# A four-layer graph network: router logits inside the normalizations, one stage for a graph layer's batch norms, attention vectors as weight columns

## The chip, the cores and the metric

The kernel runs on one core of one Trainium2 chip. The metric is the device time of one execution in microseconds (us), the median of three runs. TensorE does matrix products, VectorE (DVE in the profile), ScalarE (ACT) and GpSimd (POOL) do elementwise work, SyncE (SP) issues transfers; each runs its own list of instructions, and they wait for each other on semaphores.

## The reference, cut to what matters

The program has four layers on 3125 nodes of 256 numbers and 50000 edges. Each layer is a graph part with a mixing part, and then a feed-forward part. Only these steps are touched:

```python
def _layernorm(x, axis=-1, eps=1e-05):
    m = jnp.mean(x, axis=axis, keepdims=True)
    v = jnp.var(x, axis=axis, keepdims=True)
    return (x - m) / jnp.sqrt(v + eps)

# feed-forward of layers 0, 1, 2 (16, 8 and 8 experts): the input is _layernorm(x)
logits = xt @ Wr + br                 # then softmax, top 2, 1 or 2
# layer 2 only: the normalized rows are normalized once more for the experts
xn = (xt - mu) * jax.lax.rsqrt(var + LN_EPS)

# graph part of layer 2, x is the normalized input
y = agg + eps_weight * x
h = jax.nn.relu(_batchnorm(y @ w1.T, gamma1, beta1))     # mean and variance over the nodes
y = jax.nn.relu(_batchnorm((h @ w2.T) * n_norm, gamma_h, beta_h))
y = y + x

# graph part of layer 3
h = x @ W
s, t = h @ a[:f_out], h @ a[f_out:]
```

## The kernel before, in words

The nodes are cut into NT = 25 tiles of P = 125 rows. `R.X` holds the running sum with a node per partition, `R.XN` its normalized copy, `R.XNT` the same turned by TensorE, so that 128 of the 256 columns (KC = 2 chunks) lie on the partitions. All of these are f32. The program is a row of stages. Most of them open a `Block`, at whose end all five engines meet at a barrier; inside a block each engine follows its own list in the order written, and nothing passes a barrier.

- `normalize_stage` (L463): DVE takes `bn_stats` of each tile (or is given `moments` by the stage before), ACT takes one square root, DVE writes 25 normalized tiles (L495), TensorE turns each with two transposes (L517), ACT copies them to `XNT` (L505).
- `router_stage` (L2225) first calls `rows_stage` (L526), which loads the gate weights (L554), multiplies tile by tile (L595) and lets DVE add the bias (L2246). A second block then chooses experts, nearly all of it on DVE, with one exponential on ACT (L2284).
- Layer 2's feed-forward calls `normalize_stage` a second time (f2ln2, on `R.XN` in place, without turning) after the router and before the rows are stored for the experts (L2450).
- `isomorphism_graph_layer` (L3219): after the edge stage, one block adds eps times the input (L3240), `turn_stage` turns the sums, `batchnorm_product_stage` runs twice (loads, products of 500 columns at L3155, copy or scaling at L3172 and L3170, then 50 `bn_stats` at L3178, then the batch norm and relu on ACT in two instructions of 3125 columns, L3204), and `rows_stage` turns the result back by a product with a unit matrix and adds it and the input to `R.X` (L3268, L3270).
- `attention_graph_layer` (L3309): `rows_stage` multiplies by W, and its `finish` (L3325 to L3332) copies 256 columns out of PSUM, multiplies them twice and sums them twice on DVE, per tile; two transfers per tile store the result (L561).

Matrix products of f32 appear twice in the trace, as two weight loads (PEld) and two multiplications (PE); transposes appear once.

## Time and profile before

| | before |
|---|---|
| median of 3 runs | 6918.84 us (6914.28 to 6926.26) |
| time of the profiled execution | 6917.47 us |
| its span, first to last instruction | 6915.8 us |
| mean granted TensorE clock | 0.823 |
| busy: PE, DVE, POOL, ACT | 61%, 51%, 44%, 27% |

The profiled execution is the one whose trace is read below; its time is 1.7 us more than its span, and 1.4 us less than the median. A granted clock of 1.00 is 2.4 GHz and of 0.50 is 1.2 GHz, the two levels that TensorE has; a value between is a mean over time.

### The profile page before, as it was taken

To read this page: it belongs to the slowest core of one execution; us is meant where nothing else is said; L and a number is where in the kernel's file an instruction comes from. 1 tells how busy PE (TensorE), PEld (TensorE's weight loads), DVE (VectorE), ACT (ScalarE), POOL (GpSimd) and SP (SyncE) were. 2 spreads that over 40 slices of the span, in tenths; PEclk is the share of its full clock that TensorE was granted. 3 is DMA by queue.
4 is the path that set the end of the run, shared out by engine and by line. 5 is a ranking of instruction groups with operands and counts; after the bars stand their busy time and mean duration, and the time that the engine had idled before them with its cause. 6 is when DMAs were issued, how large, how long until landed. Compare 5 with 4: busy or idle time off the path is not lost. (4 is left out here: it accounts for less than half of the span.)

```text
span 6915.8 us, 68089 instructions
## 1 busy us (share of the span) xinstructions
PE 4214.5 (61%) x17738; PEld 2954.0 (43%) x17738; DVE 3498.8 (51%) x8540; ACT 1896.6 (27%) x4978; POOL 3013.4 (44%) x3029
## 2 busy tenths in 40 slices
PE   0023567777777499476665592555445994577659
PEld 0000334444444277134444482344325883344436
DVE  7700478888888621636554214643343113555447
ACT  0000046666666222013343121000011221244321
POOL 0777023333333055326666364666502443466520
PEclk9985688888888599689877696777676997799879
DMA  1001023333334166343336232333603663333220
GB/s 40 3 18 25 11 81 97 98 99 99 98 97 97 37 192 196 97 146 89 90 89 84 73 97 85 91 92 91 74 13 101 191 192 89 89 86 87 78 44 19
DMA packets 364930, 600.63 MB, mean 87 GB/s; under 512 B 122830, under 2 KB 248896, under 8 KB 361176
## 3 DMA queue, kind: packets, MB, share of 16 engines
q0 software_dynamic: 162496, 359.47, 21.7%
q1 hardware_dynamic: 202060, 236.87, 11.1%
q8 instruction: 151, 2.47, 0.1%
q14 instruction: 223, 1.82, 0.1%
HBM read 517.26 MB, written 78.63 MB: 86 GB/s over the span
## 5 line engine op out<-in xcount | busy, mean ns | idle before, releaser
L1675 POOL DMA_INDIRECT g0e_got<-g_table,g0e_rc x496 | 475.5, 959 | 1079.9 <-DVEq L1835 728.9
L1428 POOL DMA_INDIRECT g1e_got<-g_table,g1e_rc x496 | 492.4, 993 | 457.8 <-DMA g1e_rc<-rec_dst 218.6
L1428 POOL DMA_INDIRECT g2e_got<-g_table,g2e_rc x496 | 480.5, 969 | 279.9 <-issue 140.5
L1428 POOL DMA_INDIRECT g3e_got<-g_table,g3e_rc x440 | 432.6, 983 | 356.5 <-issue 114.0
L1484 PE MATMUL g2e_pa<-g2e_got,g2e_placew 128*125 128x256 f32 x992 | 340.2, 505 | 369.9 <-DVEq L1586 261.7
L1763 PE MATMUL g0e_spread<-g0e_expanded,g0e_by_tile 128*125 128x512 bf16 x992 | 418.7, 514 | 176.8 <-ACT g0e_spaced L1712 141.1
L2640 PE MATMUL f_p<-f_w2s,f_hid 128*128 128x256 f32 (+1 forms) x2176 | 498.8, 386 | 39.4 <-ACT f_hid L2660 31.9
L257 POOL DMA_INDIRECT rec_dst<-bydst_rc,bydst_sloti x391 | 400.1, 1023 | 274.9 <-DVEq L450 150.3
L2629 PE MATMUL f_p<-f_xt,f_w1s 128*128 128x256 f32 (+1 forms) x2176 | 495.6, 385 | 29.2 <-issue 18.7
L1712 ACT ACTIVATE g0e_spaced<-g0e_spread 125x512 bf16<-125x512 f32 x992 | 499.4, 624 | 21.0 <-issue 7.7
L2660 ACT ACTIVATE f_hid<-f_p,f_b1s 128x256 f32<-128x256 f32 (+1 forms) x544 | 248.7, 472 | 850.4 <-PE f_p L2629 442.4
L2629 PEld LDWEIGHTS f_p<-f_xt,f_w1s 128*128 128x128 f32 x2176 | 417.8, 193 | 96.9 <-issue 20.9
L2640 PEld LDWEIGHTS f_p<-f_w2s,f_hid 128*128 128x128 f32 (+1 forms) x2176 | 408.2, 191 | 116.4 <-ACT f_hid L2660 61.0
L1484 PEld LDWEIGHTS g2e_pa<-g2e_got,g2e_placew 128*125 128x125 f32 x992 | 240.4, 254 | 454.2 <-issue 408.2
L257 POOL DMA_INDIRECT rec_src<-bysrc_rc,bysrc_sloti x391 | 381.0, 974 | 119.2 <-issue 119.2
L1484 PE MATMUL g3e_pa<-g3e_got,g3e_placew 128*125 128x257 f32 x880 | 269.4, 459 | 185.6 <-ACTq L1448 119.7
L2595 POOL DMA_INDIRECT f_got<-f_rows,f_of_slot x176 | 186.1, 1058 | 386.5 <-PE f_pt L2617 290.1
L1818 DVE TENSOR_TENSOR g0e_spaced<-g0e_spaced 125x2048 bf16<-125x2048 bf16 x496 | 326.9, 659 | 54.4 <-ACT g0e_spaced L1712 7.7
L1769 PE MATMUL g0e_pa<-g0e_msg,g0e_place 128*125 128x272 f32 x992 | 335.6, 496 | 3.0 <-DVEq L1853 3.0
L1484 PE MATMUL g1e_pa<-g1e_got,g1e_placew 128*125 128x256 f32 x992 | 308.2, 465 | 11.3 <-issue 6.7
L1763 PEld LDWEIGHTS g0e_spread<-g0e_expanded,g0e_by_tile 128*125 128x125 bf16 x992 | 140.6, 152 | 406.2 <-ACT g0e_spaced L1712 367.5
L517 PE MATMUL ln_pt<-identf,XN 125*128 125x125 f32 x200 | 44.5, 367 | 440.9 <-DVE XN L495 363.2
(664 smaller groups left out, 8247.9 us busy)
## 6 DMA issues: line engine op xcount, KB each, us to landing
f_w1s<-in_L_ffn_W SPq DMA_DIRECT2D x32, 1024.0 KB
f_w2s<-in_L_ffn_W SPq DMA_DIRECT2D x32, 1024.0 KB
g_table<-g1t_out SPq DMA_DIRECT2D x25, 896.0 KB
f_w1s<-in_L_ffn_w SPq DMA_DIRECT2D x40, 512.0 KB
f_w2s<-in_L_ffn_w SPq DMA_DIRECT2D x40, 512.0 KB
f_results<-f_y SPq DMA_DIRECT2D x88, 224.0 KB
f_b2s<-in_L_ffn_b SPq DMA_DIRECT2D x80, 128.0 KB
f_w1s<-in_L_ffn_w SPq DMA_DIRECT2D x9, 1024.0 KB
```

Of the source, the lines that this page charges most:

```text
L257: pool.indirect_dma_start(self.rec, bass.IndirectOffsetOnAxis(self.sloti[:, c:c + 1], 0), self.rc[:, c, :], None).then_inc(scattered, 16)
L1428: pool.indirect_dma_start(got[:, g % GOTS, j, :], None, table, bass.IndirectOffsetOnAxis(rc[:, g * GT + j, idx:idx + 1], 0))\
L1484: last = pe.matmul(pa[x % adds][:, 0:width], placew[:, g % 3, j, :], got[:, g % GOTS, j, 0:width], start=(j % each == 0), stop=(j % each = ...
L1675: pool.indirect_dma_start(got[:, s, j, :], None, table, bass.IndirectOffsetOnAxis(rc[:, sl, j, R_IDX:R_IDX + 1], 0)).then_inc(got_in[s], 16)
L1712: act.activation(spaced[:, j, h:h + 4, :], spread[:, u % 3, :].rearrange("p (h e) -> p h e", e=128), ACT.Copy).then_inc(copied, 1)
L1763: pe.matmul(spread[:, u % 3, :], by_tile[:, j, :], expanded[:, s % 2, h:h + 4, :], start=True, stop=True).then_inc(spread_out, 1)
L1769: last = pe.matmul(pa[:, 0:W], place[:, s, j, :], msg[:, s % 2, j, :], start=(j == 0), stop=(j == GT - 1))
L1818: dve.tensor_tensor(a, a, b, ALU.max)
L2595: pool.indirect_dma_start(got[:, s % 2, j, :], None, rows, bass.IndirectOffsetOnAxis(of_slot[:, s * TJ + j:s * TJ + j + 1], 0))\
L2629: last = pe.matmul(p1[n % 4][:, 0:TS], w1s[:, weights_of(s), c, f * 128:(f + 1) * 128], xt[:, s % 2, c, :], start=(c == 0), stop=(c == KC ...
L2640: last = pe.matmul(p2[n % 2][:, 0:D], hid[:, f, j * RP:(j + 1) * RP], w2s[:, weights_of(s), f, :], start=(f == 0), stop=(f == NF - 1))
L2660: act.activation(hid[:, f, :], p1[n % 4][:, 0:TS], func, bias=b1s[:, weights_of(s), f:f + 1])\
```

## The change

Four places are rewritten.

1. `normalize_stage` can be given a `Logits` object. It then loads the gate weights itself, and TensorE multiplies tile t-2 by them right after it has turned tile t. All 25 results stay in one PSUM bank, and DVE adds the bias to all of them in one instruction. `router_stage` no longer calls `rows_stage`.
2. For layer 2 `normalize_stage` also gets `moments`, so that it takes no statistics of `R.X`, and an `Again` object: after the last normalized tile DVE takes the statistics of the normalized rows. In the router block DVE and ACT turn them into a scale and a shift, and ACT normalizes the 25 tiles a second time while DVE goes on with the router. The second `normalize_stage` (f2ln2) is gone.
3. `isomorphism_tail` does in one block what six did: TensorE turns the sums, DVE adds eps times `XNT` while it takes them out of PSUM (`join`), products, copies and `bn_stats` follow chunk by chunk (six chunks of 500 columns, one of 125), the batch norms run on ACT per chunk, and each chunk goes on to the next product at once. The result is turned back by transposes, DVE adds it to `R.X` and takes the `bn_stats` for the next normalization. The input `R.XN` is added to `R.X` by one GpSimd instruction on 6400 columns.
4. `attention_rows_stage` multiplies W by the two attention vectors once, on DVE, and puts the two sums beside W as columns 257 and 258. Per tile ACT copies 256 columns and DVE copies two single columns.

The core of the diff; removed functions stand above in full.

```diff
@@ normalize_stage
+            if again is not None:
+                dve.drain()
+                for t in range(NT):
+                    dve.bn_stats(again.stats[:, t, :], node_tile(dst, t))
+                dve.drain()
+                for t in range(NT):
+                    dve.bn_aggr(again.mv[:, t, :], again.stats[:, t, :])
+            if logits is not None:
+                E = logits.experts
+                dve.wait_ge(logits.loaded, 32)
+                dve.wait_ge(logits.multiplied, NT)
+                dve.tensor_tensor(logits.lg[:, :, :], lp[:, 0:NT * E].rearrange("p (t e) -> p t e", e=E),
+                                  logits.gb[:, :].rearrange("p (a e) -> p a e", a=1).broadcast_to([P, NT, E]), ALU.add)
...
+            def project(t):
+                pe.wait_ge(evacuated, t + 1)
+                for c in range(KC):
+                    last = pe.matmul(lp[:, t * logits.experts:(t + 1) * logits.experts], R.XNT[:, c, t * P:(t + 1) * P],
+                                     logits.gw[:, c, :], start=(c == 0), stop=(c == KC - 1))
+                last.then_inc(logits.multiplied, 1)
...
+                    turn(t)
+                    if logits is not None and t >= 2:
+                        if t == 2:
+                            pe.wait_ge(logits.loaded, 32)
+                        project(t - 2)
@@ router_stage, scalar
             act.drain().then_inc(exped, 1)
+            if again is not None:
+                act.wait_ge(again.have_var, 1)
+                act.activation(again.std[:, :], again.std[:, :], ACT.Sqrt).then_inc(again.rooted, 1)
+                act.wait_ge(again.ready, 1)
+                for t in range(NT):
+                    act.activation(node_tile(R.XN, t), node_tile(R.XN, t), ACT.Identity, bias=again.shift[:, t:t + 1],
+                                   scale=again.std[:, t:t + 1])
@@ router_stage, vector
             dve.drain().then_inc(shifted, 1)
+            if again is not None:
+                dve.tensor_scalar(again.std[:, :], again.mv[:, :, 1], LN_EPS, None, ALU.add)
+                dve.drain().then_inc(again.have_var, 1)
+                dve.wait_ge(again.rooted, 1)
+                dve.reciprocal(again.std[:, :], again.std[:, :])
+                dve.drain()
+                dve.scalar_tensor_tensor(out=again.shift[:, :], in0=again.mv[:, :, 0], scalar=-1.0, in1=again.std[:, :],
+                                         op0=ALU.mult, op1=ALU.mult)
+                dve.drain().then_inc(again.ready, 1)
             dve.wait_ge(exped, 1)
@@ isomorphism_tail (new)
+        @block.gpsimd
+        def _(pool):
+            pool.tensor_tensor(R.X[:, :], R.X[:, :], R.XN[:, :], ALU.add).then_inc(xn_added, 1)
...
+            turn(0)
+            pe.wait_ge(first_in, 48)
+            for q in range(NQ):
+                if q + 1 < NQ:
+                    turn(q + 1)
+                pe.wait_ge(joined, tiles(q)[-1] + 1)
+                if q >= 2:
+                    pe.wait_ge(a_copied, q - 1)
+                product(0, yt, q, a_made)
...
+            for q in range(NQ):
+                at = columns(q)
+                act.wait_ge(a_made, q + 1)
+                act.activation(zt[:, :, at], ps[q % 2][:, :, 0:at.stop - at.start], ACT.Copy).then_inc(a_copied, 1)
...
+            def join(q):
+                for t in tiles(q):
+                    rows = slice(t * P, (t + 1) * P)
+                    dve.wait_ge(turned, t + 1)
+                    dve.scalar_tensor_tensor(out=yt[:, :, rows], in0=R.XNT[:, :, rows], scalar=eps[:, 0:1],
+                                             in1=pt[t % 2][:, 0:KC * P].rearrange("k (c p) -> k c p", p=P),
+                                             op0=ALU.mult, op1=ALU.add).then_inc(joined, 1)
...
+            dve.wait_ge(eps_in, 16)
+            join(0)
+            for q in range(NQ):
+                if q + 1 < NQ:
+                    join(q + 1)
+                dve.wait_ge(a_copied, q + 1)
+                for m in range(KC):
+                    for t in tiles(q):
+                        dve.bn_stats(stats[:, 0, m, t, :], zt[:, m, t * P:(t + 1) * P])
...
+            moments_of(1)
+            dve.wait_ge(xn_added, 1)
+            for t in range(NT):
+                x = node_tile(R.X, t)
+                dve.wait_ge(rows_turned, t + 1)
+                dve.tensor_tensor(x, x, bk[t % 2][:, 0:D], ALU.add)
+                dve.drain().then_inc(rows_added, 1)
+                dve.bn_stats(row_stats[:, t, :], x)
@@ attention_rows_stage (new)
+        def _(act):
+            for t in range(NT):
+                act.wait_ge(multiplied, t + 1)
+                if t >= OUTS:
+                    act.wait_ge(stored[t % OUTS], 32 * (t // OUTS))
+                act.activation(out[:, t % OUTS, 0:D], ps[t % OUTS][:, 0:D], ACT.Copy).then_inc(copied, 1)
...
+            for k in range(2):
+                dve.tensor_tensor(tmp[:, k, :, :], w[:, :, 0:D],
+                                  av[:, k, :].rearrange("p (a e) -> p a e", a=1).broadcast_to([128, KC, D]), ALU.mult)
+            dve.drain()
+            for k in range(2):
+                dve.tensor_reduce(w[:, :, D + k], tmp[:, k, :, :], AX.X, ALU.add)
+            dve.drain().then_inc(folded, 1)
+            for t in range(NT):
+                dve.wait_ge(copied, t + 1)
+                if t >= OUTS:
+                    dve.wait_ge(stored[t % OUTS], 32 * (t // OUTS))
+                dve.tensor_copy(out[:, t % OUTS, D + 1:D + 2], ps[t % OUTS][:, D:D + 1])
+                dve.tensor_copy(S[:, t:t + 1], ps[t % OUTS][:, D + 1:D + 2])
+                dve.drain().then_inc(taken, 1)
```

How the order changes is seen on three lists. First TensorE in layer 0's normalization and router, before: `f0ln_pt` are the transposes, `f0r_lg_ps` the logits, the branches are ends and starts of blocks.

```order
L517 MATMUL f0ln_pt<-identf,XN 128x125 x50
L465 UNCONDITIONAL_BRANCH
L575 UNCONDITIONAL_BRANCH
L595 MATMUL f0r_lg_ps<-f0r_gw,XNT 125x16 x50
L533 UNCONDITIONAL_BRANCH
```

The same place after the change, from its start (`f0ln_lp` are the logits):

```order
L560 MATMUL f0ln_pt<-identf,XN 128x125 x6
L567 MATMUL f0ln_lp<-f0l_gw,XNT 125x16 x2
L560 MATMUL f0ln_pt<-identf,XN 128x125 x2
L567 MATMUL f0ln_lp<-f0l_gw,XNT 125x16 x2
L560 MATMUL f0ln_pt<-identf,XN 128x125 x2
```

Two transposes and two products now take turns in one block, tile by tile, where before all transposes stood ahead of a barrier and all products behind it.

Second, TensorE after layer 2's edge stage, after the change: `g2p_pt` are the transposes of the sums, `g2p_ps` the products. Before, the 50 transposes (L3092) made a block of their own ahead of all products.

```order
L3224 MATMUL g2p_pt<-identf,g_acc 128x125 x16
L3232 MATMUL g2p_ps<-g2p_yt,g2p_ws 128x500 x4
L3224 MATMUL g2p_pt<-identf,g_acc 128x125 x8
L3232 MATMUL g2p_ps<-g2p_yt,g2p_ws 128x500 x4
L3224 MATMUL g2p_pt<-identf,g_acc 128x125 x8
```

Third, DVE in the same place after the change; the first row of each pair is the joins, the second the statistics of a chunk of the product.

```order
L3285 SCALAR_TENSOR_TENSOR g2p_yt<-XNT,g2p_eps,g2p_pt 128x2x125 x8
L3313 BN_STATS g2p_stats<-g2p_zt 128x6 x8
L3285 SCALAR_TENSOR_TENSOR g2p_yt<-XNT,g2p_eps,g2p_pt 128x2x125 x4
L3313 BN_STATS g2p_stats<-g2p_zt 128x6 x8
L3285 SCALAR_TENSOR_TENSOR g2p_yt<-XNT,g2p_eps,g2p_pt 128x2x125 x4
```

The joins of chunk q+2 now stand behind the statistics of chunk q on DVE, while the transposes of chunk q+2 stand ahead of the product of chunk q+1 on TensorE.

## Rows read from the trace of the kernel before

**Rows 1.** Busy time by stretch: start:end us, length, busy (instructions), granted clock.

```profile
core 0: us, PE busy (x) PEld busy (x) DVE busy (x) ACT busy (x) POOL busy (x), PEclk, DMA share, GB/s
2329.00:2334.00 5.00, 4.74 (x23) 3.90 (x24) 5.00 (x17) 3.70 (x10) 0.00 (x0) 0.50 0.00 0
2342.70:2364.00 21.30, 21.18 (x100) 21.07 (x100) 4.24 (x25) 0.00 (x0) 0.00 (x0) 0.50 0.00 0
...
5028.00:5048.00 20.00, 18.83 (x51) 8.81 (x49) 7.96 (x14) 0.00 (x0) 0.00 (x0) 1.00 0.00 0
5882.00:5930.00 48.00, 26.10 (x76) 15.32 (x76) 40.80 (x133) 0.00 (x0) 0.00 (x0) 0.85 0.21 60
```

**Rows 2.** Timeline of layer 0's normalization and logits: start, length, instructions, [idle before].

```profile
2329.26 6.00 PEld L517 LDWEIGHTS f0ln_pt<-identf,XN 125*128 125x128 f32 x30 [15.75 <-DVE XN L495]
...
2342.74 21.18 PE L595 MATMUL f0r_lg_ps<-f0r_gw,XNT 128*125 128x16 f32 x100 [3.94 <-DMA f0r_gb<-in_L_ffn_gate_b]
...
2363.96 0.17 DVE L2246 TENSOR_TENSOR f0r_lg<-f0r_lg_ps,f0r_gb 125x16 f32<-125x16 f32 x1 [0.67 <-PE f0r_lg_ps L595]
```

**Rows 3.** Timeline of layer 2's graph part behind the edge stage, into the normalization.

```profile
5000.07 9.99 DVE L3240 SCALAR_TENSOR_TENSOR g_acc<-XN,g_eps,g_acc  x25 [4.16 <-DMA g_eps<-in_L_gnn_eps_weight]
...
5023.25 23.58 PE L3155 MATMUL g2a_ps<-g_yt,g2a_ws 128*128 x56 [4.12 <-DVEq L3164]
...
5029.33 1.26 DVE L3172 COPY g_zt<-g2a_ps 128x500 f32 x2 [19.27 <-PE g2a_ps L3155]
...
5032.68 1.27 DVE L3172 COPY g_zt<-g2a_ps 128x500 f32 x2 [2.08 <-PE g2a_ps L3155]
...
5048.59 0.54 DVE L3178 BATCH_NORM_STATS2 g2a_stats<-g_zt  x2 [0.47 <-issue]
...
5068.05 0.83 DVE L3183 BATCH_NORM_AGGREGATE g2a_mv<-g2a_stats 128x2 f32<-128x150 f32 x1
...
5070.36 5.87 ACT L3204 ACTIVATE g_zt<-g_zt,g2a_shift,g2a_scale 128x3125 f32<-128x3125 f32 x2 [0.97 <-DVEq L3196]
...
5166.41 0.42 DVE L3268 TENSOR_TENSOR X<-X,g2back_ps 125x256 f32<-125x256 f32 x1
5166.91 0.43 DVE L3270 TENSOR_TENSOR X<-X,XN 125x256 f32<-125x256 f32 x1
...
5169.56 8.26 DVE L485 BATCH_NORM_STATS2 f2ln_stats<-X 125x6 f32<-125x256 f32 x25 [1.18 <-PEq L3583]
...
5180.85 8.16 DVE L495 TENSOR_SCALAR XN<-X,f2ln_mv,f2ln_std 125x256 f32<-125x256 f32 x25
```

**Rows 4.** Timeline of layer 2's router and the second normalization behind it.

```profile
5221.48 0.23 ACT L2284 ACTIVATE f_weight<-f2r_diff 125x25 f32<-125x25 f32 x1 [4.16 <-DVEq L2329]
...
5221.76 0.18 DVE L2333 TENSOR_SCALAR f_weight<-f_weight 125x25 f32<-125x25 f32 x1 [0.34 <-ACTq L2287]
...
5222.94 0.64 DVE L2344 COPY f2r_totals<-f2r_ps 125x200 f32<-125x200 f32 x2 [0.34 <-PE f2r_ps L2296]
...
5231.84 1.28 ACT L501 ACT_TABLE_LOAD   x1 [10.13 <-PEq L2232]
...
5251.35 5.50 SPq L2450 DMA_DIRECT2D f_rows<-XN  x2
```

**Rows 5.** ACT and POOL groups: line engine op, shapes, count | busy, mean ns | idle.

```profile
L3456 ACT ACTIVATE f_hid<-f_p,f_b1s 128x500 f32<-128x500 f32 x48 | 32.4, 677 | 120.0 <-PE f_p L3434 120.0
...
L786 ACT ACTIVATE m_k<-m_sq,m_rk 125x256 f32<-125x256 f32 x25 | 12.5, 499 | 0.0
...
L318 POOL IOTA sort_gid<- 128x496 f32 x1 | 0.6, 550 | 17.3 <-POOLq L3558 17.3
```

**Rows 6.** Instructions of line L561: count, min/median/max ns, first to last start.

```profile
L561 SPq DMA_DIRECT2D g_table<-g3h_out x50: 308/354/393, 5878.2 to 5929.3; - x50
```

**Rows 7.** Timeline of layer 3's product with W and of the stage behind it.

```profile
5873.97 7.39 PE L595 MATMUL g3h_ps<-g_w,XNT 128*125 128x258 f32 x24 [6.08 <-DMA g_a<-in_L_gnn_a]
...
5931.36 1.77 SPq L1414 DMA_DIRECT2D g3e_rc<-rec_src  x4
```

More of the change, by code:

```diff
@@ L478, in normalize_stage, with _ @@
             "have_var", "have_std", "normed", "turned", "evacuated"))
+        if logits is not None:
+            lp = ctx.enter_context(nc.psum_tensor(f"{name}_lp", [P, 512], F32))
         block = open_block(nc, R, ctx)
+        if logits is not None:
+            @block.sync
+            def _(sp):
+                sp.dma_start(logits.gw[:, :, :], chunks_of(logits.gate_w, logits.experts)).then_inc(logits.loaded, 16)
+                sp.dma_start(logits.gb[:, :], row_of(logits.gate_b, P)).then_inc(logits.loaded, 16)
+                sp.wait_ge(logits.loaded, 32)
         @block.vector
@@ L2237, in sem @@
             return nc.alloc_semaphore(f"{name}_{n}")
-        gw = sb("gw", [128, KC, experts])
-        gb = sb("gb", [P, experts])
-        lg = sb("lg", [P, NT * experts])
-        lgv = lg[:, :].rearrange("p (t e) -> p t e", e=experts)
+        lgv = logits.lg[:, :, :]
         best = sb("best", [P, top, NT])
-        def finish(dve, t, ps, out):
-            dve.tensor_tensor(lg[:, ds(t * experts, experts)], ps[:, 0:experts], gb[:, :], ALU.add)
-        rows_stage(nc, R, f"{name}_lg", gw[:, :, :], experts, finish,
-                   loads=[(gw[:, :, :], chunks_of(gate_w, experts)), (gb[:, :], row_of(gate_b, P))])
         items = top * NT
@@ L3305, in third_feed_forward, with attention_rows_stage, sb, _ @@
         routed_experts_stage(nc, R, "f2", F2, a["L2_ffn_W1"], a["L2_ffn_b1"], a["L2_ffn_W2"], a["L2_ffn_b2"], route,
                              ACT.Gelu, ThirdSettle(nc, ctx, R, route, moments), ln=a["L2_ffn_ln"], spare=spare, share=5)
+def attention_rows_stage(nc, R, a, S, table):
+    with ExitStack() as ctx:
+        def sb(n, shape):
+            return ctx.enter_context(nc.sbuf_tensor(f"g3h_{n}", shape, F32))
+        w, av, tmp = sb("w", [128, KC, D + 2]), sb("av", [128, 2, D]), sb("tmp", [128, 2, KC, D])
+        out = sb("out", [P, OUTS, D + 2])
+        ps = [ctx.enter_context(nc.psum_tensor(f"g3h_ps{k}", [P, 512], F32)) for k in range(OUTS)]
+        loaded, folded, multiplied, copied, taken = (nc.alloc_semaphore(f"g3h_{n}") for n in (
+            "loaded", "folded", "multiplied", "copied", "taken"))
+        stored = [nc.alloc_semaphore(f"g3h_stored{k}") for k in range(OUTS)]
+        block = ctx.enter_context(nc.Block())
+        @block.sync
+        def _(sp):
+            sp.dma_start(w[:, :, 0:D], chunks_of(a["L3_gnn_W"], D)).then_inc(loaded, 16)
+            sp.dma_start(av[:, 0, :], row_of(a["L3_gnn_a"][D:2 * D], 128)).then_inc(loaded, 16)
+            sp.dma_start(av[:, 1, :], row_of(a["L3_gnn_a"][0:D], 128)).then_inc(loaded, 16)
+            sp.wait_ge(loaded, 48)
+            for t in range(NT):
+                sp.wait_ge(taken, t + 1)
+                for own in spans(P):
+                    sp.dma_start(table[t * P:(t + 1) * P, :][own, :], out[own, t % OUTS, :]).then_inc(stored[t % OUTS], 16)
+            for k in range(OUTS):
+                sp.wait_ge(stored[k], 32 * len(range(k, NT, OUTS)))
+        @block.tensor
+        def _(pe):
+            pe.wait_ge(folded, 1)
+            for t in range(NT):
+                if t >= OUTS:
+                    pe.wait_ge(taken, t - OUTS + 1)
+                for c in range(KC):
+                    last = pe.matmul(ps[t % OUTS][:, 0:D + 2], R.XNT[:, c, t * P:(t + 1) * P], w[:, c, :], start=(c == 0),
+                                     stop=(c == KC - 1))
+                last.then_inc(multiplied, 1)
+        @block.scalar
+        def _(act):
+            for t in range(NT):
+                act.wait_ge(multiplied, t + 1)
+                if t >= OUTS:
+                    act.wait_ge(stored[t % OUTS], 32 * (t // OUTS))
+                act.activation(out[:, t % OUTS, 0:D], ps[t % OUTS][:, 0:D], ACT.Copy).then_inc(copied, 1)
+        @block.vector
+        def _(dve):
+            dve.memset(out[:, :, D:D + 1], 1.0)
+            dve.wait_ge(loaded, 48)
+            for k in range(2):
+                dve.tensor_tensor(tmp[:, k, :, :], w[:, :, 0:D],
+                                  av[:, k, :].rearrange("p (a e) -> p a e", a=1).broadcast_to([128, KC, D]), ALU.mult)
+            dve.drain()
+            for k in range(2):
+                dve.tensor_reduce(w[:, :, D + k], tmp[:, k, :, :], AX.X, ALU.add)
+            dve.drain().then_inc(folded, 1)
+            for t in range(NT):
+                dve.wait_ge(copied, t + 1)
+                if t >= OUTS:
+                    dve.wait_ge(stored[t % OUTS], 32 * (t // OUTS))
+                dve.tensor_copy(out[:, t % OUTS, D + 1:D + 2], ps[t % OUTS][:, D:D + 1])
+                dve.tensor_copy(S[:, t:t + 1], ps[t % OUTS][:, D + 1:D + 2])
+                dve.drain().then_inc(taken, 1)
```

341 lines of the change are left out of this document (160 added, 181 removed).

## The prediction

> **What bounds the kernel now.** No engine is busy for more than 61% of the span, and stages end at barriers that nothing passes, so the share of an engine says little: a change is worth what it takes off the chain inside its own stage. I read, in this order, the busy times by stretch for the clock [rows 1], then the timeline of each of the four places [rows 2, 3, 4, 7], then groups by line for prices that these places do not show [rows 5, 6]. The reader is to see three kinds of lost time. In the logits TensorE is never idle, yet it runs at 1.2 GHz (granted 0.50) over 21.3 us [rows 1]. Behind layer 2's edge stage one engine works while the others stand: product, then statistics, then relu, then the next product. In layer 3's product with W, TensorE is busy for 26.1 of 48 us and DVE for 40.8 [rows 1]: DVE is the bound.
>
> The sum is made against the profiled execution, 6917.5 us, which is 1.4 us under the median.
>
> **Term 1, logits in the normalization (three layers).** Layer 0 before: first transpose at 2329.26, last bias add ends at 2364.13, so 34.9 us, with the wait for the gate weights and a barrier inside [rows 2]. After: one stream on TensorE of 50 transposes and 100 load-and-multiply pairs (the f32 products count twice). At 1.2 GHz a transpose costs 6.00/30 = 0.20 us and a pair 21.18/100 = 0.21 us [rows 2]; the granted clock was 0.50 over both [rows 1]. 50 x 0.20 + 100 x 0.21 = 31.2 us, then one bias add over 400 columns, between the 0.17 of 16 columns [rows 2] and the 0.63 of 500 columns [rows 3]; I take 0.5 and 0.1 for the handover: 31.8 us. Saved 3.1 us per layer, **9.3 us** in all. From both sides: nothing saved if each turn from transpose to product costs 0.1 us more, and 16 us each if the clock rises (a rival below). Layer 2's extra statistics (25 at 0.33 [rows 3] and 25 small ones) lie under this stream, which outlasts the normalized tiles (8.2 us) by 23 us: nothing.
>
> **Term 2, the tail of layer 2's graph part.** Before: from the landing of eps at 5000.07 to the first normalized tile of the next stage at 5180.85, 180.8 us [rows 3]. After, counted from the same landing:
>
> - Joins of the first two chunks: 8 at 0.40 (9.99/25 [rows 3]) if nothing waits; two PSUM buffers go back and forth between TensorE and DVE, so 3.7.
> - First product: 6.1 cold (5023.25 to 5029.33), 3.35 warm (5029.33 to 5032.68) [rows 3]; the 16 transposes ahead warm it partly: 5.0.
> - Now the order on the two lists makes a chain. Product q, copy of 1000 columns on ACT (500 take 0.68 [rows 5], so 0.68 to 1.35; I take 1.1), 8 statistics (0.54 for two [rows 3], 2.0), two joins (0.9), two transposes (0.3), handovers (0.3): 4.6 us in which TensorE has only transposes. Only then comes product q+1. This repeats four times; the fifth chunk follows at once, as its joins are already made.
> - The products 1 to 4 take 3.35 each warm. A stretch in which TensorE is 54% busy had a mean clock of 0.85 [rows 1], so 3.95 is taken: 4 x (4.6 + 3.95) = 34.2. Then product 3.35, copy 1.1, statistics 2.0 and the short chunk 0.5: 7.0. The sum so far is 49.9.
> - Moments: 5068.05 to 5070.36 is 2.3 from the last aggregate to the relu [rows 3], with a second aggregate of 0.83 ahead: 3.1. Relu starts at 53.0; before it started at 70.3.
> - Second half: relu of one chunk 1.4 (2 x 0.68 [rows 5]; the two old ones of 3125 columns gave 5.87 [rows 3]), first product cold 6.1, then six chunks at the larger of 3.35 on TensorE and 1.27 + 0.1 + 2.0 = 3.4 on DVE [rows 3], 20.4, and the short chunk 1.1: 29.0. Moments 3.1, relu and first turn 2.0: 87.1. Gone are the second load wait and the wait for the whole relu.
> - Rows: add and drain 0.50 (5166.41 to 5166.91), statistics 0.33 (8.26/25) to 0.43 [rows 3]; I take 0.9 for both, 22.5 for 25. Aggregates, root, reciprocal: 3.0 (5169.56 + 8.26 to 5180.85), barrier 1.2 [rows 3]. First normalized tile at 113.9.
>
> Saved 180.8 - 113.9 = **66.9 us**. Bounds: 75 if the products stay warm and the gaps shrink to 3.5; 52 if all products of the first half run at 1.2 GHz (6.1 each, 9 more) and the second half loses as much in part. GpSimd's add of 6400 columns is unpriced by any row of its kind; one of 496 columns takes 0.55 [rows 5], 7 us by that measure, and it has 87 us until DVE asks for it: nothing (a rival below). The 1.5 MB load of the norm row is issued at the start and needed at 54: nothing.
>
> **Term 3, the second normalization on ScalarE.** Removed is all from 5231.84 to 5251.35, 19.5 us [rows 4]. Added on DVE's chain: before, it went on at 5221.76, after the exponential [rows 4]. Now it waits until ACT has ended it, loaded the table for the root (1.28 [rows 4]) and taken the root (0.23 like the exponential), and then makes a reciprocal and a shift (0.7): 2.2 us later, less the 0.3 it waited for TensorE at 5222.94 anyway [rows 4]: 1.9. What queues behind this wait on DVE is the rest of the router, 10 us. ACT starts the 25 tiles at 5224.0. One costs 0.50 alone [rows 5]; in a row they overlap a little, and I take 0.42, 10.5 us, so ACT ends at 5234.5 where DVE ends at 5233.5. The barrier comes 3.0 us later than before. Saved 19.5 - 3.0 = **16.5 us**; bounds 14.5 (0.50 a tile) to 17.6 (DVE is last).
>
> The Trainium skill (ScalarE: Activation LUTs, What ACT_TABLE_LOAD costs) puts a switch of table sets at about 2.66 us, half of it a drain, which speaks against placing a root between exponentials. By it the term would be 15.1 us; the row shows 1.28 for the load, and no row here shows the drain.
>
> **Term 4, layer 3's product with W.** Before: 5873.97 to the next stage's first issue at 5931.36, 57.4 us [rows 7]. After: the folding is four DVE instructions of 512 columns at 0.65 (1.26/2 for 500 [rows 3]), with drains 2.8. Per tile TensorE has four products of 258 columns (24 for six tiles [rows 7]); eight of 500 take 3.35 warm [rows 3], so 0.42 for 500, 0.22 for 258, 0.87 a tile warm and 1.73 cold. SP issues two transfers per tile, 0.31 and 0.39 [rows 6], 0.8 with its waits, under that. The four buffers come round after copy 0.4, DVE 0.5, issues 0.8 and landing about 1.3: 3.0/4 = 0.75, under it too. So TensorE sets the pace: cold for about 4.5 us (2.6 tiles), 22.4 tiles at 0.87 = 19.5, the last copy and issue 1.3, last issue to next stage 2.1 (5929.3 to 5931.36 [rows 6, 7]): 30.2. Saved 27.2, and 0.2 for a block that is gone: **27.4 us**. Bounds: 29 (warm from the start) to 20 (1.2 us a tile if landing is slower under twice the traffic).
>
> **Sum.** 9.3 + 66.9 + 16.5 + 27.4 = 120.1. 6917.5 - 120.1 = 6797.4, or **6799** as a median.
>
> **The rivals.**
>
> *The clock rises in the logits (0.10).* The stream now has transposes among the products, and transposes alone ended at full clock: pairs of them take 0.20 us early and less later. If it rises after 5 us in each layer, the other 26 us halve, 13 us x 3: 6760. Against it: TensorE was busy without a hole and stayed at 0.50 [rows 1], and the transposes are now a third of the stream. The Trainium skill (TensorE: Matmul & The Clock Gate, What's actually happening) says that the gate goes by how busy TensorE has been of late; by that rule the stream would rise. The row disagrees for loads with 16 columns each.
>
> *The chains are slower than priced (0.22).* Every product of the tail's first half cold (6.1 for 3.95, 9 us) and layer 3 at 1.1 us a tile (5 us): 6813. For it: TensorE has gaps of 4.6 us there. Against it: 0.85 in a stretch with such gaps [rows 1].
>
> *GpSimd's add is late: slower than before (0.02).* DVE waits for it ahead of the first row. From 90 us on it delays the end, and from 210 us, 33 ns a column, the kernel is slower; at 40 ns it takes 256 us, and the time is 6965. Against it: 1.1 ns a column [rows 5].
>
> **How the numbers follow.** The forecast has 0.66, with its own range of 6785 to 6812. The range 6764 to 6830 leaves out the GpSimd case, most of the risen clock and the far end of the slow chains, together under 2 in 10. All cases but one end over 80 us below 6919, so faster by over 0.2% (14 us, about what this measurement can tell from no change) has 0.97, within 0.2% 0.01, slower 0.02.
>
> **What would show each step.** Term 1: the granted clock over the mixed stream is 0.50 and it lasts 31 us; wrong if 1.00 appears. Term 2: products of the first half start every 8 to 9 us with ACT, DVE and transposes between; the second half every 3.4; GpSimd's add ends long before the rows. Term 3: a table load inside the router, DVE idle near 2 us there, 25 ACT tiles ending within 1.5 us of DVE's last. Term 4: stores 0.87 us apart and PE busy in one block. The forecast fails if a chain not named here sets one of these stages, above all in the first half of term 2, the largest sum of unseen handovers.

## The result and the profile after

The kernel after takes 6802.44 us (median of 3, 6802.25 to 6804.22), against 6918.84 before: a ratio of 0.9832 (95% interval 0.9812 to 0.9851). 6799 was forecast, within 6764 to 6830. The profiled execution took 6804.22 us, its span 6802.5, the mean granted clock 0.823 as before.

Both traces cut at the same marks, in us. The last two columns are a second pair of the same two kernels, profiled in later sessions (the first and the last run below).

| stage | before | after | saved | before, again | after, again |
|---|---|---|---|---|---|
| layer 0, normalization to dispatch | 71.0 | 66.0 | 5.0 | 71.2 | 66.0 |
| layer 1, the same | 57.5 | 52.5 | 5.0 | 57.3 | 52.5 |
| layer 2, end of edge part to first normalized tile | 184.9 | 117.2 | 67.7 | 185.9 | 115.4 |
| layer 2, first normalized tile to dispatch | 70.5 | 51.5 | 19.1 | 70.8 | 51.5 |
| layer 3, product with W, first issue to next stage's | 62.4 | 37.4 | 25.0 | 62.5 | 36.1 |
| not touched: layer 0's experts | 381.0 | 392.1 | -11.1 | 380.4 | 388.7 |
| not touched: layer 2's experts | 526.8 | 522.0 | 4.8 | 526.9 | 522.6 |
| not touched: layer 3's edge part | 769.1 | 775.4 | -6.4 | 756.6 | 761.7 |
| not touched: all else | 4792.6 | 4788.4 | 4.2 | 4765.0 | 4762.6 |
| span | 6915.8 | 6802.5 | 113.3 | 6876.7 | 6757.0 |

The five stages that the change touches give 121.8 us, where 120.1 was forecast. The others give 8.5 back, where the forecast had nothing.

Busy times of the kernel after by stretch, columns as in [rows 1]: layer 0's mixed stream, the tail's first and second half, layer 3's product.

```profile
2335.00:2355.00 20.00, 20.00 (x106) 20.00 (x104) 1.91 (x6) 6.47 (x17) 0.00 (x0) 0.50 0.00 1
5003.00:5046.00 43.00, 32.21 (x87) 15.59 (x86) 15.89 (x59) 5.03 (x5) 7.30 (x1) 0.83 0.06 22
5053.00:5077.00 24.00, 23.18 (x56) 10.85 (x56) 15.04 (x52) 9.07 (x13) 0.00 (x0) 0.89 0.00 0
5781.00:5809.00 28.00, 24.12 (x100) 19.81 (x100) 6.11 (x51) 9.53 (x25) 0.00 (x0) 0.92 0.38 108
```

In the logits TensorE is busy for 20.00 of 20 us and still granted 0.50. The second half of the tail and layer 3 run at the upper level for most of the time (0.89 and 0.92 in the mean).

The timeline of the kernel after in the four places, to be held against [rows 2, 3, 4, 7].

```profile
2329.20 1.51 PE L560 MATMUL f0ln_pt<-identf,XN 125*128 125x125 f32 x6 [15.47 <-DVE XN L526]
...
2331.27 0.66 PE L560 MATMUL f0ln_pt<-identf,XN 125*128 125x125 f32 x2
...
2331.73 0.86 PE L567 MATMUL f0ln_lp<-f0l_gw,XNT 128*125 128x16 f32 x4
...
2332.43 0.66 PE L560 MATMUL f0ln_pt<-identf,XN 125*128 125x125 f32 x2
...
2358.60 0.57 DVE L539 TENSOR_TENSOR f0l_lg<-f0ln_lp,f0l_gb 125x400 f32<-125x400 f32 x1 [21.70 <-PE f0ln_lp L567]
...
4996.58 13.71 POOL L3215 TENSOR_TENSOR X<-X,XN 125x6400 f32<-125x6400 f32 x1 [21.00 <-POOLq L1434]
...
4999.31 0.86 DVE L3285 SCALAR_TENSOR_TENSOR g2p_yt<-XNT,g2p_eps,g2p_pt 128x250 f32<-128x250 f32 x2 [5.00 <-DMA g2p_eps<-in_L_gnn_eps_weight]
...
5003.28 5.38 PE L3232 MATMUL g2p_ps<-g2p_yt,g2p_ws 128*128 128x500 f32 x8
...
5008.70 1.01 ACT L3267 ACTIVATE g2p_zt<-g2p_ps 128x1000 f32<-128x1000 f32 x1 [419.06 <-PE g2p_ps L3232]
5009.73 1.62 DVE L3313 BATCH_NORM_STATS2 g2p_stats<-g2p_zt 128x6 f32<-128x125 f32 x8 [5.73 <-ACT g2p_zt L3267]
5011.27 1.85 DVE L3285 SCALAR_TENSOR_TENSOR g2p_yt<-XNT,g2p_eps,g2p_pt 128x250 f32<-128x250 f32 x4
...
5011.78 0.82 PE L3224 MATMUL g2p_pt<-identf,g_acc 125*128 125x125 f32 x4 [2.70 <-DVE g2p_yt L3285]
...
5012.44 3.52 PE L3232 MATMUL g2p_ps<-g2p_yt,g2p_ws 128*128 128x500 f32 x8
...
5019.74 5.22 PE L3232 MATMUL g2p_ps<-g2p_yt,g2p_ws 128*128 128x500 f32 x8
...
5052.20 10.49 ACT L3275 ACTIVATE g2p_zt<-g2p_zt,g2p_shift,g2p_scale 128x500 f32<-128x500 f32 x14 [0.97 <-DVEq L3303]
...
5085.93 0.42 DVE L3333 TENSOR_TENSOR X<-X,g2p_bk 125x256 f32<-125x256 f32 x1 [2.54 <-PE g2p_bk L3259]
...
5111.51 8.16 DVE L526 TENSOR_SCALAR XN<-X,moments,f2ln_std 125x256 f32<-125x256 f32 x25
...
5141.71 0.37 DVE L539 TENSOR_TENSOR f2l_lg<-f2ln_lp,f2l_gb 125x200 f32<-125x200 f32 x1 [11.84 <-PE f2ln_lp L567]
...
5147.79 0.22 ACT L2337 ACTIVATE f_weight<-f2r_diff 125x25 f32<-125x25 f32 x1 [4.17 <-DVEq L2389]
...
5148.10 1.28 ACT L2343 ACT_TABLE_LOAD   x1
...
5149.65 0.32 DVE L2394 RECIPROCAL f2a_std<-f2a_std 125x25 f32<-125x25 f32 x1 [1.62 <-ACT f2a_std L2343]
...
5150.31 12.39 ACT L2346 ACTIVATE XN<-XN,f2a_shift,f2a_std 125x256 f32<-125x256 f32 x25 [0.69 <-DVEq L2398]
...
5159.54 0.21 DVE L2487 SCALAR_TENSOR_TENSOR f_low<-f_high,f_slot 125x50 f32<-125x50 f32 x1
...
5162.95 5.49 SPq L2519 DMA_DIRECT2D f_rows<-XN  x2
...
5790.65 0.39 ACT L3434 ACTIVATE g3h_out<-g3h_ps 125x256 f32<-125x256 f32 x1 [0.49 <-PE g3h_ps L3424]
...
5792.18 0.38 ACT L3434 ACTIVATE g3h_out<-g3h_ps 125x256 f32<-125x256 f32 x1 [1.15 <-DMA g_table<-g3h_out]
```

A tile of logits takes 1.16 us (2331.27 to 2332.43). In the tail the joins of a chunk (5011.27) follow the statistics (5009.73) of the chunk before, and the next product follows the joins: the first five products start 7.3 to 9.2 us apart, 9.16 us in the first pair shown. In the router VectorE's last instruction ends at 5159.75, ScalarE's 25 tiles only at 5162.70. In layer 3 ScalarE waits first for TensorE (0.49) and then, from the ninth tile on, for stores.

### The profile page after: what moved, and what is told of

Its sections match the earlier page's. It is cut to its first block and busy times, and to the rows that moved or that the text cites. A ratio compares the mean times of both kernels' runs of the same rounds, so it can differ in the third digit from the quotient of the medians.

```text
span 6802.5 us, 67183 instructions
## 1 busy us (share of the span) xinstructions
PE 4214.7 (62%) x17688; PEld 2957.8 (43%) x17688; DVE 3417.9 (50%) x8306; ACT 1926.3 (28%) x5034; POOL 3024.5 (44%) x3030
## 5 line engine op out<-in xcount | busy, mean ns | idle before, releaser
L257 POOL DMA_INDIRECT rec_src<-bysrc_rc,bysrc_sloti x391 | 381.0, 974 | 119.2 <-issue 119.2
L1545 PE MATMUL g1e_pa<-g1e_got,g1e_placew 128*125 128x256 f32 x992 | 308.3, 465 | 10.2 <-DMA g1e_got<-g_table,g1e_rc 5.1
```

The costliest lines, as they stand in the source:

```text
L257: pool.indirect_dma_start(self.rec, bass.IndirectOffsetOnAxis(self.sloti[:, c:c + 1], 0), self.rc[:, c, :], None).then_inc(scattered, 16)
L1545: last = pe.matmul(pa[x % adds][:, 0:width], placew[:, g % 3, j, :], got[:, g % GOTS, j, 0:width], start=(j % each == 0), stop=(j % each = ...
```

## The experiments

The kernel before took 6918.84 us in the first session and 6875.57, 6873.01, 6878.60 and 6916.40 in the later ones, so each time stands against its own session's, and stages are compared by profiles. A time without a range is that of one run.

**The kernel before, again.** 

> The kernel before, run once more. It asks whether stages that the change does not touch vary by themselves. Layer 0's experts, from the issue of the row store to the first instruction of the combination, took 381.0 us before and 392.1 after; layer 3's edge part, from its first issue to the next normalization, 769.1 before and 775.4 after. Theory (these stages wait for transfers, and the waits differ from one execution to the next): at least one of the two lies 3 us or more from its time before. Rival (the change lengthens them, by where its tensors come to lie or when its transfers start): both within 1 us of 381.0 and 769.1 here, and near 392 and 775 in every kernel built from the one after.

6878.37 us. Layer 0's experts 380.4, layer 3's edge part 756.6. The second varies by itself (12.5 us); the first does not. The theory holds for the one, and the rival stays for the other.

**Four buffers for the tail's transposes** (kernel after):

```diff
-        pt = [... f"g2p_pt{k}" ... for k in range(2)]
+        pt = [... f"g2p_pt{k}" ... for k in range(4)]
-        bk = [... f"g2p_bk{k}" ... for k in range(2)]
+        bk = [pt[k][0:P, :] for k in range(2)]
-                    if t >= 2:
-                        pe.wait_ge(joined, t - 1)
+                    if t >= 4:
+                        pe.wait_ge(joined, t - 3)
```

> In the tail of layer 2's graph part the transposes get four PSUM buffers instead of two, so that TensorE can turn the tiles of chunk q+1 ahead of product q without waiting for joins that stand behind statistics. Theory (the gap of some 4.5 us between two products of the first half is the order on two lists and two buffers, not the work): the first five products start 4.2 to 4.6 us apart instead of 7.3 to 9.2, and the tail from the first join to the first normalized tile of the next stage goes from 112.2 to 94 to 97 us. Rival (the gap is work of ScalarE and VectorE for each chunk, copy 1.0, statistics 1.6, joins 1.9 us, which only moves): products still 6 us or more apart, 104 us or more. In both the other three places stay as they are.

6739.45 us, session's before 6875.57. Tail 97.7 us from the end of the edge part, against 115.4 to 117.2: 18 us less. Timeline of this kernel:

```profile
4966.64 1.63 DVE L3285 SCALAR_TENSOR_TENSOR g2p_yt<-XNT,g2p_eps,g2p_pt 128x250 f32<-128x250 f32 x4 [3.52 <-DMA g2p_eps<-in_L_gnn_eps_weight]
...
4975.60 3.52 PE L3232 MATMUL g2p_ps<-g2p_yt,g2p_ws 128*128 128x500 f32 x8
...
4978.95 1.02 PE L3224 MATMUL g2p_pt<-identf,g_acc 125*128 125x125 f32 x8
...
4979.81 3.52 PE L3232 MATMUL g2p_ps<-g2p_yt,g2p_ws 128*128 128x500 f32 x8
...
4980.19 1.62 DVE L3313 BATCH_NORM_STATS2 g2p_stats<-g2p_zt 128x6 f32<-128x125 f32 x8 [1.06 <-ACT g2p_zt L3267]
...
5001.61 10.49 ACT L3275 ACTIVATE g2p_zt<-g2p_zt,g2p_shift,g2p_scale 128x500 f32<-128x500 f32 x14 [0.97 <-DVEq L3303]
```

Products start 4.21 us apart (4975.60, 4979.81), and the relu comes 35.0 us after the first join instead of 52.9. Copy, statistics and joins take what they took; they now lie beside the products. The gap was order and two buffers.

**The second normalization inside the first one's block.**

```diff
 # normalize_stage, vector, behind the second moments
+                dve.tensor_scalar(again.std[:, :], again.mv[:, :, 1], LN_EPS, None, ALU.add)
+                dve.drain().then_inc(again.have_var, 1)
+                dve.wait_ge(again.rooted, 1)
+                dve.reciprocal(again.std[:, :], again.std[:, :])
+                dve.drain()
+                for t in range(NT):
+                    dve.wait_ge(turned, t + 1)
+                    dve.tensor_scalar(node_tile(dst, t), node_tile(dst, t), again.mv[:, t, 0:1], again.std[:, t:t + 1],
+                                      ALU.subtract, ALU.mult)
 # scalar, ahead of copy 18: the square root;  router_stage without again
```

> Layer 2's second normalization moves out of the router into the first normalization's block: the square root after ScalarE's eighteenth copy, and the 25 tiles on VectorE, each behind its two transposes. Theory (TensorE's stream of transposes and logits sets that block, and VectorE stands idle from 5129.9 to its end at 5141.0; in the router ScalarE's 25 tiles at 0.495 us end last, 3 us behind VectorE, and the root holds VectorE for 2 us): the block stays at 30.4 to 31.2 us from its first normalized tile to the router, the router falls from 20.6 to 15.3 to 16.0 us, so 4.6 to 5.3 us less. Rival (VectorE's extra tiles slow the copies or the transposes through the shared memory, or the last tiles hang over the stream's end): the block grows by 3 us or more and under 2 us is left.

6763.15 us, before 6875.57. Timeline of this kernel:

```profile
5099.48 8.17 DVE L543 TENSOR_SCALAR XN<-XN,f2a_mv,f2a_std 125x256 f32<-125x256 f32 x25
5109.03 0.37 DVE L549 TENSOR_TENSOR f2l_lg<-f2ln_lp,f2l_gb 125x200 f32<-125x200 f32 x1 [1.39 <-PE f2ln_lp L580]
```

First normalized tile to dispatch 46.5 us instead of 51.5; the block keeps its length. The theory holds: VectorE's 8.17 us of tiles lie in its idle time, of which 1.39 us are left before the bias add where the kernel after has 11.84. But layer 2's experts took 527.1 us, not 522, so in all the 5 us were not seen (below).

**Wide products that nobody reads.**

```diff
 # tensor, ahead of the transposes: 32 in layers 0 and 1, none in layer 2
+                    pe.matmul(sink[:, :], wide[:, 0:128], wide[:, :], start=True, stop=True)
 # in project(t): none in layer 0, one in layers 1 and 2
+                    pe.matmul(sink[:, :], wide[:, 0:128], wide[:, :], start=True, stop=True)
```

> Useless products of 512 bf16 columns are added around the logits: in layers 0 and 1 32 of them while VectorE takes the statistics, in layer 1 one more for each tile, in layer 2 none ahead and one for each tile. The stream of two transposes and four 16- or 8-column products takes 1.155 us a tile at a granted clock of 0.50. Theory (the level depends on how much TensorE streams, and a stream that is begun at the upper level may hold it): layer 0's stream begins at 1.00, and if it holds it a tile takes 0.58 us; layer 1 holds it, 0.8 us a tile, 9 us less than 28.9; layer 2's stays at 0.50 and costs 1.58 us a tile, 10.7 us more. Rival (the level follows from how busy TensorE is, and 100% busy at 0.50 means that the level is given from elsewhere): no layer rises in its stream, layer 0 is as before, layers 1 and 2 pay 10.7 us each.

6756.14 us, before 6875.57. By stretch, one of the statistics and one or two of the stream for each of layers 0, 1 and 2:

```profile
2314.71:2319.71 5.00, 4.16 (x20) 1.67 (x17) 4.92 (x32) 0.00 (x0) 0.00 (x0) 1.00 0.00 0
...
2324.71:2329.71 5.00, 5.00 (x27) 5.00 (x28) 4.54 (x15) 1.52 (x4) 0.00 (x0) 0.50 0.01 3
...
3810.76:3815.76 5.00, 5.00 (x45) 4.76 (x45) 4.55 (x15) 2.28 (x6) 0.00 (x0) 1.00 0.02 5
3815.76:3820.76 5.00, 5.00 (x45) 4.76 (x45) 0.00 (x0) 2.28 (x6) 0.00 (x0) 1.00 0.00 0
...
5079.07:5084.07 5.00, 5.00 (x24) 4.53 (x24) 5.00 (x16) 1.14 (x3) 0.00 (x0) 0.50 0.00 0
```

TensorE is busy for 5.00 of 5 us in all three streams. Layer 0's began at 1.00 and fell to 0.50; layer 1's, with one wide product in a tile, kept 1.00 and did 45 instructions where layer 0's did 27; layer 2's, with the same product in each tile but begun at 0.50, never rose. (Layer 0 with one a tile was run below, and gains as layer 1 does.) Normalization to dispatch: layer 0 65.1 (0.9 less), layer 1 44.4 (8.1 less), layer 2 61.6 from the first tile (10.2 more). The Trainium skill (TensorE: Matmul & The Clock Gate, What's actually happening) puts the gate down to how busy the engine has been; by that rule all three streams would have stood at 1.00, and the rows disagree for two of them.

**Attention vectors alone.** The kernel before, with `attention_rows_stage` in place of the folding, the product and the four VectorE instructions a tile. 

> The kernel before with the fourth place alone: attention vectors as weight columns. Two questions. First, is its gain its own: from the first issue of that stage to the first issue of layer 3's edge part 62.4 us before, 37.4 after. Theory: 35 to 38 us here too, no matter what the other three places do. Second, why layer 0's experts take 388 to 392 us in every kernel built from the one after and 380.4 to 381.0 in both runs of before, with the 2048-byte packets of their weights at 108 to 114 ns against 101 to 102. Theory A (it comes from layer 0's own rewriting, 5 us earlier or other instructions ahead of it): 380 to 382 us here. Theory B (any other program has its instructions or inputs elsewhere in memory, and the weights' packets meet other traffic): it moves here too, to 385 us or more, though nothing ahead of it is changed.

6853.83 us, before 6873.01. The stage takes 35.4 us: the gain of 25 to 27 is its own. Layer 0's experts 380.2, so theory B, put for any other program, falls.

**Layer 0's logits taken out again.**

```diff
-            normalize_stage(nc, R, "f0ln", R.X, R.XN, logits=logits)
+            normalize_stage(nc, R, "f0ln", R.X, R.XN)
+            rows_stage(nc, R, "f0r_lg", logits.gw[:, :, :], E0, finish, loads=[...])
```

> The kernel after with layer 0's logits taken out of the normalization again: the products behind a barrier as before, one bias add for each tile. Theory (the first term is worth 5 us a layer, of which 3.2 come from the barrier and the load wait and the rest from transposes and products that take 1.155 us a tile instead of 1.26): normalization to dispatch of layer 0 goes back from 66.0 to 70.5 to 71.5 us, layer 1 stays at 52.5. Rival (the gain is the single bias add): 67 us. For layer 0's experts: theory A (its own rewriting lengthens them): back to 380 to 382 us. Theory B (placement of program or data): anything, most likely still 385 us or more.

6753.75 us, before 6873.01. 68.1 us, between theory and rival. Most of the difference to before stands in the clock. By stretch from the first normalized tile on, in the second run of before:

```profile
2320.76:2326.76 6.00, 5.48 (x27) 4.39 (x28) 5.95 (x19) 4.39 (x12) 0.00 (x0) 0.53 0.00 0
```

and in this kernel:

```profile
2320.67:2326.67 6.00, 5.48 (x30) 4.03 (x30) 5.95 (x19) 4.59 (x14) 0.00 (x0) 0.71 0.00 0
```

The transposes were granted 0.71 over these 6 us here, 0.53 there. Later the router's counting products ran at the upper level here (the last two took 0.83 us, 1.54 there), which shortens the router by 1.4 us. In the run with the tail alone, where layer 0 is untouched, it was 0.71 too, and the stage took 68.1. So the unchanged stage varies from 68.1 to 71.2. The changed one varies as well: 66.0 with the router's products at 0.50, 64.6 in the run with the logits alone, where they rose. Like against like, this place is worth 3.5 to 5 us. Layer 0's experts stay at 388.7: theory A falls.

**The improvements together** (the kernel with three, in the expectations). The four buffers, the early second normalization, 32 wide products ahead and one a tile in layers 0 and 1, none in layer 2, and eight buffers (`OUTS`) in layer 3. 

> What the experiments so far point to, put together in the kernel after: four PSUM buffers for the transposes in the tail, the second normalization inside the first one's block, 32 useless wide products during the statistics and one for each tile in the logits of layers 0 and 1 (none in layer 2), and eight buffers instead of four in layer 3's product with W. Theory (the gains are in separate stages and add up): against the kernel after 8 us in each of layers 0 and 1, 18 in the tail, 5 in the second normalization, 2 to 3 in layer 3, 41 in all; the ratio to the kernel before goes from 0.983 to 0.975 to 0.979. In layer 3 ScalarE waits for no store any more and TensorE sets the pace at 0.87 us a tile. Rival (what is saved ahead of the experts is given back as longer waits for weights, and the stores in layer 3 land no faster with more buffers): 30 us or less of it remains, ratio 0.979 or above.

6723.92 us (6719.88 to 6763.78), ratio 0.9791 (0.9766 to 0.9816). Against the second profile of the kernel after (the last run below) the touched stages give 8.1, 8.1, 17.9, 5.2 and 1.2, 40.6 us, as forecast; the untouched ones took 15.5 back in the profile, of which layer 3's edge part 7.0 and layer 2's experts 4.1. So for the whole kernel the rival's figures came: 25.1 us are left by the profiles, and the ratio is at its 0.979, just outside the theory's range. Whether the untouched stages drifted or answered the change is open. Groups of layer 3's product in this kernel, and what its engines waited for:

```profile
L3448 PE MATMUL g3h_ps<-g3h_w,XNT 128*125 128x258 f32 x100 | 24.0, 405 | 7.9 <-DVEq L3470 7.9
...
L3458 ACT ACTIVATE g3h_out<-g3h_ps 125x256 f32<-125x256 f32 x25 | 9.6, 384 | 22.4 <-PE g3h_ps L3448 22.4
```

ScalarE waits for TensorE alone; in the first profile of the kernel after 9.4 us of its waits were for stores:

```profile
L3434 ACT ACTIVATE g3h_out<-g3h_ps 125x256 f32<-125x256 f32 x25 | 9.5, 385 | 24.4 <-PE g3h_ps L3424 14.7 <-DMA g_table<-g3h_out 9.4 <-issue 0.3
```

All its waits together are only 2.0 us shorter with eight buffers (22.4 for 24.4), since without waits for stores it waits for TensorE more often. And the stage itself scatters by more than that: 34.9, 36.3 and 36.6 us in the three kernels with eight buffers, 35.0 to 37.4 in the seven profiles with four. The 1.2 us are not shown to be the buffers' gain.

**Layer 2's logits at the upper level too** (the kernel with four). Added are wide products in the tail's last nine tiles, eight behind them, two ahead of the normalization and one a tile; ScalarE takes the second normalization's last ten tiles. 

> As the kernel with three upper-level changes, and layer 2's logits too: wide products between the last nine row transposes of the tail and eight behind them, two at the start of the normalization, one for each tile; the second normalization's last ten tiles on ScalarE, since VectorE alone would now end last. Theory (a stream that begins at the upper level and holds one wide product a tile stays there): layer 2's stream is granted 1.00 and takes 0.79 us a tile instead of 1.155, and its block from the first normalized tile to the router 24 to 26 us instead of 31; 5 to 6 us less than the kernel with three. Rival (the wide products at the end of the tail come too late or too thinly to raise the level): granted 0.50, 1.58 us a tile, 41 us, 9 to 11 us slower than the kernel with three.

6731.87 us (6721.57 to 6758.52), ratio 0.9809 (0.9790 to 0.9829). The rival's figures came, 57.9 us to dispatch and the stream at 0.50, but not for its reason. The wide products had raised the level: it stood at 1.00 from 5038 to 5043, and TensorE was idle for 3.56 us of that, from 5040.0 on.

**The same with the border bridged**, 20 wide products for 8 and 10 for 2. 

> As the kernel with four upper-level places, but the idle stretch between the tail's last product and the next stage's first is bridged: 20 wide products instead of 8 behind the last row transposes, 10 instead of 2 at the start of the normalization. In the kernel with four the level stood at 1.00 from 5036 to 5043, TensorE then idled for 3.56 us across the stage's border, and the stream behind it ran at 0.50. Theory (the level was lost in that idle stretch): layer 2's stream is granted 1.00, and from the first normalized tile to dispatch 39 to 42 us instead of 57.9; 5 to 7 us less than the kernel with three, ratio 0.975 to 0.980. Rival (the mixed stream of layer 2 cannot hold the upper level, 8 columns a product instead of layer 1's 8 too, but with VectorE's statistics beside it): granted 0.50 again, 56 to 59 us.

6767.53 us (6750.50 to 6797.36), before 6916.40: 0.9791 (0.9769 to 0.9813). 45.7 us where 39 to 42 were forecast, and the ratio is that of the kernel with three: the 5 to 7 us are not seen. The idle stretch at the border is 1.74 us now, the level held across it, and something else gave way. By stretch from the border on, and the timeline at the fall:

```profile
5077.22:5082.22 5.00, 4.94 (x43) 4.76 (x44) 4.90 (x16) 2.28 (x6) 0.00 (x0) 1.00 0.01 3
5082.22:5087.22 5.00, 5.00 (x44) 4.75 (x43) 5.00 (x16) 2.28 (x6) 0.00 (x0) 1.00 0.01 2
5087.22:5092.22 5.00, 3.55 (x29) 3.07 (x28) 4.67 (x35) 0.87 (x3) 0.00 (x0) 1.00 0.00 0
5092.22:5097.22 5.00, 4.57 (x25) 4.22 (x26) 4.34 (x14) 2.06 (x7) 0.00 (x0) 0.66 0.02 5
```

```profile
5092.11 0.23 ACT L568 ACTIVATE f2a_std<-f2a_std 125x25 f32<-125x25 f32 x1 [3.55 <-DVEq L542]
...
5092.65 0.60 PE L595 MATMUL f2ln_lp<-f2l_gw,XNT 128*125 128x8 f32 x4 [1.83 <-ACT XNT L570]
```

At 1.00 TensorE reaches tile 18 before VectorE has the second moments. The square root stands ahead of that copy on ScalarE's list and holds it for 3.55 us, TensorE idles for 1.83 us, and the last tiles run at 0.50. This stretch is hardly longer than the 1.74 us at the border, where the level held, so the length of an idle stretch alone does not tell when the level falls. The faster stream turned a cover into a wait. A root two or three tiles later was not run.

**The tail alone, and the logits alone** (kernel before with one place each). 

> The kernel before with the third place alone: one block for layer 2's tail, its row statistics handed to the next normalization. Theory (the tail's gain is its own): from the end of layer 2's edge part to the first normalized tile 115 to 119 us, as after (117.2), where before has 184.9; some 67 us less in all. Rival (part of it belongs to the logits or the second normalization, which change the stage behind it): 125 us or more. It is also half of a search for what lengthens layer 0's experts from 380.4 to 388 us: 385 us or more here would put it on the tail's code, which runs 2600 us later and can reach layer 0 only through where the program or its data lie; 380 to 382 us would leave the logits of layers 1 and 2.

6811.61 us, before 6878.60: 67.0 us less, as forecast, with the tail at 113.5 us, a little under its range. 

> The kernel before with the first place alone: logits inside the normalization in layers 0, 1 and 2, layer 2's second normalization still a stage of its own. Theory (4.3 to 5 us a layer, whatever the rest does): normalization to dispatch 65.5 to 66.5 in layer 0 and 52 to 53 in layer 1, and in layer 2 76.5 to 78 us instead of 81.8 to 82.1. For layer 0's experts the other half of the search: 385 us or more puts the loss on the logits of layers 1 and 2, or on all three; 380 to 382 us on none of them.

6865.01 us, before 6878.60: 64.6, 52.5 and, to dispatch in layer 2, 76.8 us. The first is under its range by the level of the router's products (above). Both gains are each place's own. Layer 0's experts 381.5 and 381.4.

**The kernel after, again.** 

> The kernel after, unchanged, on the chip on which the other kernels ran, so that they can be set against it. Theory: stage by stage as in its first profile, within 0.5 us in the four places; layer 0's experts 387 to 392 us; ratio to the kernel before 0.981 to 0.985, 6745 to 6765 us. Against it the kernel with three upper-level changes gains 30 us or more. Rival (the combined kernel's gain is drift between runs): the kernel after comes out at 6735 us or less.

6761.53 us (6758.73 to 6763.92), before 6878.60: 0.9830 (0.9814 to 0.9847). The stages are in the first table; the tail and layer 3 differ from the first profile by 1.8 and 1.3 us, more than the 0.5 forecast, the others by 0.1 or less. Layer 0's experts took 388.7, as forecast. The kernel with three gains 25.1 us on this profile, not 30.

## Why the prediction was right, step by step

**Term 1** was forecast at 9.3 and is 14.4 us: 5.0, 5.0 and 4.4 (the logits block of layer 2, 35.2 to 30.9 from first normalized tile to router). The mechanism stood: one stream, granted 0.50. Its size was off, since the six instructions of a tile take 1.16 us, 0.193 each, where 0.20 and 0.21 had been read from separate streams. (0.20 us is the price of one transpose at 0.50; the rival's text gives it to a pair.) The rival of a rising clock did not come; with useless products paid for, the upper level was worth 8.1 us in layer 1, where the rival had 13.

**Term 2** was forecast at 66.9 and is 67.7 from the end of the edge part, 68.6 from the landing of eps, as the forecast counts. From the landing of eps the relu came at 52.9 (forecast 53.0), the first row add at 86.6 (87.1), the first normalized tile at 112.2 (113.9). Inside the first half two terms erred against each other: the gap between products is 3.8 us in the mean (forecast 4.6), and products 1 to 4 take 3.5 to 5.2, 4.6 in the mean (3.95). That the four rounds come to 33.8 us for 34.2 is luck in both sizes; the order of the chain was right. GpSimd's add took 13.71 us, twice the 7 of the forecast, and ended some 75 us before VectorE asked: off the path at either size. The third rival is out.

**Term 3** was forecast at 16.5 and is 14.7. VectorE's router grew by the 1.9 us forecast (15.5 to 17.4), and the wait for the root shows as 1.62 us idle. But ScalarE's 25 tiles took 12.39 us, 0.496 each, not 0.42: the price of one alone [rows 5], which the bounds held, was right, and ScalarE ends 3 us behind VectorE. The Trainium skill (ScalarE: Activation LUTs, What ACT_TABLE_LOAD costs) gives 186 ns + 0.833 ns an element, 93 more for each pointer operand and an overlap of 93: 492 ns estimated for 256 elements and two pointers, which the trace bears out. The drain that the Trainium skill adds there to a table load does not show: from the end of the exponential (5148.01) to the reciprocal behind the root are 1.64 us, the load of 1.28 included.

**Term 4** was forecast at 27.4 and is 25.0. TensorE set the pace, at 0.50 for 3.7 us (4.5 forecast) and then 0.87 us a tile up to the eighth; then stores came late. A turn of a buffer was priced at 3.0 us. By the landings in the trace, from the start of ScalarE's copy to the last packet of its tile 2.8 to 3.1 us passed in the first four tiles and 3.7 in the mean of all 25; in the run with the attention vectors alone it was 3.0, and only 0.6 us of waits were for stores. Here 9.4 us were, but most of them stood in place of waits for TensorE: against the kernel with eight buffers, at 0.87 to the end, they cost 2.0 us, most of the 2.4 that are missing.

**The sum.** The terms miss by +5.1, +0.8, -1.8 and -2.4 us. That they come to 121.8 for 120.1 is in part luck: the mechanisms stood, and the errors in their sizes cancel.

**What had no term.** Layer 0's experts are 11.1 us longer in the first profile and 8.3 in the second pair. In fourteen profiles (before, after and the twelve runs) they took 380.2 to 381.5 us with the kernel before and with one place alone, and 386.6 to 392.1 in all others, that with layer 0's logits taken out among them. What goes with it: the 40 loads of the experts' first weights, 512 KB each in packets of 2048 bytes, last 2.1 to 2.2 us in the mean from first to last packet in the former and 2.6 to 2.7 in the latter, and TensorE waits longer for weights there. No instruction of this stage differs. Neither layer 0's own rewriting nor any of the three places that were run alone makes it (the second place was not); whether two together do, or where the program or its data lie in memory, stays open. Layer 2's experts vary between 522 and 527 us, the whole difference ahead of the first result; its cause is open too.

## What to carry to other kernels

Price a chain by its handovers, and read from two lists which instruction stands ahead of which: here the order "joins behind statistics", with two buffers, cost 18 us, and two more buffers took them away without moving an instruction. Check what a faster stage overtakes: a root placed for a slow stream stalled the fast one. And keep a line in the sum for stages that nothing touches: they moved by 8.5 us here, five times the error of the priced terms' sum (1.7).

## What was not expected of the hardware

- The logits' stream of transposes and narrow products kept TensorE busy for 20.00 of 20 us and was granted 0.50, 1.2 GHz. With one useless product of 512 columns a tile, begun at the upper level, it stayed at 1.00, 2.4 GHz, and was faster: 0.8 us a tile for 1.16.
- In the run with four upper-level places the level was gone behind an idle stretch of 3.56 us across a stage's border. With more wide products on both sides and 1.74 us of idle time it held; which of the two did it was not run apart.
- The kernel before took 6873 to 6919 us by session, and most of the difference lies in the edge parts: 26 of the 39 us between its two profiles, of which layer 3's (769.1 and 756.6 us) gives 12.5.
